# Moving the first attention's exponential to the eviction of the transposed scores, its maximum to GpSimd and its row sums to TensorE

## The reference

```python
Q = inputs @ Wq
K = inputs @ Wk
score = jnp.einsum('bqd,bkd->bqk', Q, K) / jnp.sqrt(jnp.float32(D))
score = jnp.where(causal, score, 0.0)
score = jnp.where(score != 0, score, NEG_FILL)   # finfo(float32).min
attn = jax.nn.softmax(score, axis=-1)
V = inputs @ (Wvdown @ Wvup)
return attn @ V
```

## Time and profile before

| what | value |
|---|---|
| median of 3 runs | 1756.0 us (1753.08 to 1756.61) |
| the profiled execution | 1755.23 us, span 1753.9 us |
| mean granted clock of TensorE in it | 0.977 |
| busy: PE / DVE / ACT / POOL | 1606.6 / 1491.6 / 1368.5 / 673.2 us |

### The profile page before, as it was taken

How to read it: one execution, slowest core, us unless ns; L and a number is a source line. 1 busy time by engine, 2 the same in 40 slices (tenths; PEclk the granted TensorE clock), 3 DMA queues, 4 the chain that set the end, 5 groups by cost and what they waited for, 6 DMA issues and landing times.

```text
span 1753.9 us, 54932 instructions
## 1 busy us (share of the span) xinstructions
PE 1606.6 (92%) x23271; PEld 662.3 (38%) x23281; DVE 1491.6 (85%) x2256; ACT 1368.5 (78%) x1934; POOL 673.2 (38%) x1085
## 2 busy tenths in 40 slices
PE   5768999999999999999999999999999999998998
PEld 2543343334334343334334343334433343222224
DVE  4648988899889988899889988899888988898973
ACT  4442688987899778887899878887798878786885
POOL 2321344435534454435454364434555262002010
PEclk9997799999999999999999999999999999998999
DMA  2120211112210311112210221112111222101111
GB/s 72 50 69 21 60 41 41 36 50 64 64 53 15 98 53 54 30 43 75 66 38 28 81 66 52 33 47 75 46 40 34 63 58 64 34 25 48 35 28 35
DMA packets 83281, 87.10 MB, mean 50 GB/s; under 512 B 9452, under 2 KB 67484, under 8 KB 83036
## 3 DMA queue, kind: packets, MB, share of 16 engines
q1 hardware_dynamic: 82492, 83.07, 16.1%
q10 hardware_dynamic: 544, 0.52, 0.1%
HBM read 61.02 MB, written 21.99 MB: 47 GB/s over the span
## 4 chain that ended last, share of the span: by engine, by line
PE 60%; ACT 18%; DVE 13%; issue 4%; SPq 2%; DMA 2%; POOL 1%; ACTq 0%; POOLq 0%
PE pv_psum L836 20%; PE side_psum L564 14%; ACT p L1049 11%; PE buffer L821 11%; DVE row_max L1367 7%; PE buffer L811 7%; PE side_psum L654 2%; PE buffer L564 2%; SPq L539 2%; PE side_psum L621 1%; ACT s L965 1%; ACT o_sb L1058 1%; DVE st_f L1112 1%; ACT hT_b L1038 1%; DVE s L1215 1%
## 5 line engine op out<-in xcount | busy, mean ns | idle before, releaser
L1367 DVE TENSOR_REDUCE row_max<-buffer 128x2 f32<-128x1024 f32 x1024 | 1234.3, 1219 | 150.0 <-PE buffer L811 137.8
L1049 ACT ACTIVATE p<-buffer 128x1024 f32<-128x1024 f32 x1024 | 1044.9, 1025 | 202.0 <-PE buffer L821 187.5
L836 PE MATMUL pv_psum<-p,v 128*9 128x256 f32 x8192 | 589.8, 384 | 10.5 <-ACT o_sb L1058 9.3
L811 PE MATMUL buffer<-k_ops,q_ops 24*128 24x512 f16 x2048 | 404.8, 392 | 35.9 <-ACT p L1049 26.1
L821 PE MATMUL buffer<-q_ops,k_ops 26*128 26x512 f16 x2048 | 401.3, 388 | 12.0 <-DVE row_max L1367 7.7
L836 PEld LDWEIGHTS pv_psum<-p,v 128*9 128x9 f32 x8192 | 150.0, 89 | 245.2 <-issue 162.0
L821 PEld LDWEIGHTS buffer<-q_ops,k_ops 26*128 26x128 f16 x2048 | 96.4, 91 | 382.2 <-issue 220.8
L1498 POOL TENSOR_TENSOR hm<-masks,hT_f 128x1024 f32<-128x1024 bf16 x56 | 120.3, 2148 | 103.1 <-PE side_psum L564 99.4
L811 PEld LDWEIGHTS buffer<-k_ops,q_ops 24*128 24x128 f16 x2048 | 96.6, 91 | 163.9 <-ACT p L1049 131.1
L1513 POOL TENSOR_SCALAR nm_parts<-nm 128x16 f16<-128x16 f32 x64 | 13.2, 207 | 298.1 <-DVE nm L1292 297.8
L564 PE MATMUL side_psum<-we,hm 128*32 128x128 f32 x3648 | 121.1, 274 | 2.4 <-issue 2.4
(11 more groups left out here) (309 smaller groups left out, 1617.6 us busy)
## 6 DMA issues: line engine op xcount, KB each, us to landing
masks<-masks_rows SPq DMA_DIRECT2D x16, 1024.0 KB, 6.3
q_ops<-products SPq DMA_DIRECT2D x256, 48.0 KB
k_ops<-products SPq DMA_DIRECT2D x256, 48.0 KB
attention<-o_sb SPq DMA_DIRECT2D x248, 18.0 KB
x<-in_L_attn_inputs SPq DMA_DIRECT2D x8, 512.0 KB, 4.4
products<-q_parts SPq DMA_DIRECT2D x16, 256.0 KB, 2.3
w_sb<-in_L_ffn_W SPq DMA_DIRECT2D x16, 256.0 KB, 3.3
out<-x SPq DMA_DIRECT2D x16, 256.0 KB, 2.4
```

Of the source, the lines that this page charges most:

```text
L811: m = e.matmul(buffer[:, hh, :], q_ops[rows, slot, of, i * P:(i + 1) * P], k_ops[rows, slot, of, halves(half)[1]], start=True, stop=True)
L836: m = e.matmul(pv_psum[q:q + VW, half * QUARTER:(half + 1) * QUARTER], v1[b % 2][:, kb, 2 * hp + hh, :], p_sb[n % KEPT][:, hh, part * QUAR ...
L1049: e.activation(p_sb[n % KEPT][:, :, :], unit("exp", n)[0][:, :, :], ACT.Exp, scale=over_scale[n // (2 * PERIOD)]).then_inc(S["exp_done"], 1)
L1367: e.tensor_reduce(mx[pair % 2][:, :, i, half], unit("max", n)[0][:, :, :], axis=AX.X, op=ALU.max).then_inc(S["max_done"], 1)
```

## The change

- `exp0` leaves ACT for all batches but the first. POOL does min(s - nm0, 1000) in place instead, and ACT's copy of the transposed block into `p0T` becomes exp(-x) of it. Batch 0 keeps ACT's exponential, without the sum.
- PE sums the rows: in `times_v`, for every key block and every 32 queries, a 128x32 weight of `p0T` is multiplied with a column of ones, into column 128 of the bank. Tiles 0 and 1, which use fewer than four column tiles, get matmuls with a column of zeros for the rest. `low` has 129 columns, and its copy takes all rows.
- `sums0` takes that column on POOL, in three operations instead of two, where nm0 shows that all was masked also the keys beyond. It now comes after `times_v` of tile 3 and 7 instead of after `exp0`.
- `exp0` has a gap of 2 steps instead of 1 and is no longer in `ON_ACT`.

Left out of the diff: the orders by hand of batches 0 and 1, from which `sums0` is moved in the same way, names of semaphores, memsets, and three waits of DVE's statistics for buffers that are long free.

```diff
@@ -90,9 +91,9 @@
             out += [(1, ("softmax", n - 1))]
         if n >= 3:
-            out += [(0, ("times_v", n - 3))] + ([(2, ("up", n // 7))] if n - 3 in (3, T - 1) else [])
+            out += [(0, ("times_v", n - 3))] + ([(0, ("sums0", n // 7)), (2, ("up", n // 7))] if n - 3 in (3, T - 1) else [])
         if 1 <= n < T + 1:
-            out += [(1, ("exp0", n - 1))] + ([(0, ("sums0", n // 5))] if n in (4, T) else [])
+            out += [(2, ("exp0", n - 1))]
         if n < T:
             out += [(0, ("scores", n, c)) for c in range(len(chunks(n)))]
@@ -138,7 +139,7 @@
 ZERO_TEST_ON_DVE = 2
 ON_DVE = {"stats", "softmax", "up", "wg", "top", "index", "onehot", "over_gating", "wff", "wout_mm", "stats_b", "ffn", "maxima"}
-ON_ACT = {"exp0", "gating"} | {name for name, by in EMPTIED_BY.items() if by == "act"} - {"nm"}
+ON_ACT = {"gating"} | {name for name, by in EMPTIED_BY.items() if by == "act"} - {"nm"}
 
 FRONT_FROM, WEIGHTS_FROM, BACK_FROM, LOAD_BEFORE = -200, 90, 132, 11
@@ -662,15 +663,21 @@
                 q = COLUMN_TILE * (j % 4)
                 weight, moving = (v0_later[:, i, :], pT[:, 0, :]) if k is None else (v0[:, k, :], pT[:, k + 1, :])
-                m = e.matmul(o[q:q + COLUMN_TILE, 0:P], weight, moving, start=j < 4, stop=j + 4 >= len(some))
+                e.matmul(o[q:q + COLUMN_TILE, 0:P], weight, moving, start=j < 4, stop=j + 4 >= len(some))
+            pe.wait_ge(S["zero_column"], 1)
+            for j in range(len(some), 4):
+                q = COLUMN_TILE * j
+                e.matmul(o[q:q + COLUMN_TILE, 0:P], zero_column[:, :].broadcast_to([P, COLUMN_TILE]), pT[:, 1, :], start=True, stop=True)
+            for k in range(i + 1):
+                for q in range(0, P, COLUMN_TILE):
+                    m = e.matmul(o[q:q + COLUMN_TILE, P:P + 1], pT[:, k + 1, q:q + COLUMN_TILE], ones_column[:, :], start=k == 0, stop=k == i)
             m.then_inc(S["side_filled"], 1)
 
...
             emptied("times_v", b, 4 * half + 3)
             pe.wait_ge(S["up_weights"], b + 1)
-            pe.wait_ge(S["low_zero"], 2)
-            four(v, lambda j: low[:, 4 * half + j, :], wvub[:, :])
+            four(v, lambda j: low[:, 4 * half + j, 0:P], wvub[:, :])
 
         def wg_stage(b, half):
@@ -944,10 +951,11 @@
 
         def times_v(b, i):
-            v, rows = filled("times_v", b, i), COLUMN_TILE * min(4, len(terms(i)))
+            v = filled("times_v", b, i)
             if b:
                 act.wait_ge(S["side_filled"], side["up", b - 1, i // 4].filled)
-            e.copy(low[0:rows, i, :], v[0:rows, 0:P]).then_inc(S["side_act"], 1)
+                act.wait_ge(S[f"over_sums0_{i // 4}"], b)
+            e.copy(low[:, i, :], v[:, 0:P + 1]).then_inc(S["side_act"], 1)
 
         def scores(b, i, c):
@@ -958,22 +966,23 @@
 
         def exp0(b, i):
+            if b:
+                return
             s, n = s0_of(b, i)[0], (i + 1) * P
             start = P if i == T - 1 else 0
             act.wait_ge(S["nm0"], b * T + i + 1)
-            act.wait_ge(S[f"over_sums0_{i // 4}"], b)
-            e.activation(s[:, start:P + n], s[:, start:P + n], ACT.Exp, scale=-1.0, bias=nm0[:, i:i + 1], accum_out=acc0[:, i:i + 1]).then_inc(S["p0"], 1)
-            if i % 4 == 3:
-                tiles = halves(i // 4)[0]
-                act.wait_ge(S["low_zero"], 2)
-                e.activation(e0[:, tiles], nm0[:, tiles], ACT.Exp, bias=neg[:, :]).then_inc(S[f"sums0_{i // 4}"], 1)
+            e.activation(s[:, start:P + n], s[:, start:P + n], ACT.Exp, scale=-1.0, bias=nm0[:, i:i + 1]).then_inc(S["p0"], 1)
 
         def transpose_p(b, i, c):
...
             if min(before) >= 0:
                 act.wait_ge(S["side_filled"], side["times_v", *before].filled)
-            e.copy(pT[:, some[0]:some[-1] + 1, :].rearrange("p k q -> p (k q)"), v[:, 0:len(some) * P]).then_inc(S["side_act"], 1)
+            pT = pT[:, some[0]:some[-1] + 1, :].rearrange("p k q -> p (k q)")
+            if b == 0:
+                e.copy(pT, v[:, 0:len(some) * P]).then_inc(S["side_act"], 1)
+                return
+            e.activation(pT, v[:, 0:len(some) * P], ACT.Exp, scale=-1.0).then_inc(S["side_act"], 1)
 
         def gating(b, half, part):
@@ -1436,12 +1449,14 @@
         def sums0(b, half):
             tiles = halves(half)[0]
-            pool.wait_ge(S[f"sums0_{half}"], b + 1)
-            pool.wait_ge(S["low_zero"], 2)
+            pool.wait_ge(S["nm0"], b * T + 4 * half + 4)
+            pool.wait_ge(S["low_zero"], 1)
             if b:
                 pool.wait_ge(S["side_dve"], side["up", b - 1, half].emptied)
-            after(e.tensor_tensor(rs0[:, tiles], e0[:, tiles], beyond[:, tiles], op=ALU.mult))
-            e.tensor_tensor(rs0[:, tiles], rs0[:, tiles], acc0[:, tiles], op=ALU.add).then_inc(S[f"over_sums0_{half}"], 1)
+            after(e.tensor_scalar(rs0[:, tiles], nm0[:, tiles], -NEG, 0.0, ALU.is_equal, ALU.add))
+            after(e.tensor_tensor(rs0[:, tiles], rs0[:, tiles], beyond[:, tiles], op=ALU.mult))
+            pool.wait_ge(S["side_act"], side["times_v", b, 4 * half + 3].emptied)
+            e.tensor_tensor(rs0[:, tiles], rs0[:, tiles], low[:, tiles, P], op=ALU.add).then_inc(S[f"over_sums0_{half}"], 1)
 
         def parts(b, w, half):
@@ -1480,6 +1495,14 @@
                 e.tensor_scalar(rest[:, 0:n], s[:, P:P + n], 0.0, -NEG, ALU.is_equal, ALU.mult).then_inc(S["masked"], 1)
 
+        def exp0(b, i):
+            if b == 0:
+                return
+            s, n = s0_of(b, i)[0], (i + 1) * P
+            start = P if i == T - 1 else 0
+            pool.wait_ge(S["nm0"], b * T + i + 1)
+            e.tensor_scalar(s[:, start:P + n], s[:, start:P + n], nm0[:, i:i + 1], NO_WEIGHT, ALU.subtract, ALU.min).then_inc(S["p0"], 1)
+
         def top(b, half, part):
             if not part:
```

More of the change, by code:

```diff
@@ L27 @@
 EPS = 1e-5
+NO_WEIGHT = 1000.0
 NEG = float(np.finfo(np.float32).min)
@@ L196 @@
 scores 0 1 0, softmax 0 0, exp0 0 0, stats 0 0 0 1, softmax 0 1, transpose_p 0 0 0, later 0, scores 0 2 0, exp0 0 1, times_v 0 0, transpose_p 0 1 0,
[L197 to L198 removed]
+softmax 0 2, scores 0 3 0, exp0 0 2, times_v 0 1, transpose_p 0 2 0, softmax 0 3, scores 0 4 0, exp0 0 3, scores 0 4 1, transpose_p 0 3 0,
+transpose_p 0 3 1, scores 0 5 0, exp0 0 4, softmax 0 4, scores 0 5 1, times_v 0 2, times_v 0 3, sums0 0 0, transpose_p 0 4 0, transpose_p 0 4 1, softmax 0 5,
 up 0 0, scores 0 6 0, exp0 0 5, stats 0 1 0 0, scores 0 6 1, times_v 0 4, stats 0 1 0 1, transpose_p 0 5 0, softmax 0 6, scores 0 7 0,
 transpose_p 0 5 1, exp0 0 6, scores 0 7 1, times_v 0 5, stats 1 0 0 0, transpose_p 0 6 0, channels 0 1 0, apply 0 1 0, softmax 0 7,
[L201 to L202 removed]
+transpose_p 0 6 1, exp0 0 7, wg 0 0, times_v 0 6, stats 1 0 0 1, transpose_p 0 7 0, top 0 0 0, stats 1 0 1 0, index 0 0 0,
+transpose_p 0 7 1, top 0 0 1, stats 1 0 1 1, times_v 0 7, sums0 0 1, index 0 0 1, squares 0, onehot 0 0, gating 0 0 0, up 0 1, gating 0 0 1, stats 0 1 1 0, apply 1 0 0,
 stats 0 1 1 1, onehotT 0 0, masks_out 0 0, over_gating 0 0, channels 0 1 1, apply 0 1 1, hm 0 0, apply 1 0 1, channels 1 0 0, limits 0, wg 0 1, inverse 0, top 0 1 0,
@@ L209 @@
 scores 1 2 0, channels 0 2 1, transpose_p 1 1 0, qk1 0 0 1, apply 0 2 1, softmax 1 2, parts 0 0 1, qk1 0 1 1, scores 1 3 0, v1 0 1, exp0 1 2,
-parts 0 1 1, transpose_p 1 2 0, times_v 1 1, sums0 1 0, exp0 1 3, scores 1 4 0, scores 1 4 1, transpose_p 1 3 0, transpose_p 1 3 1, softmax 1 3,
+parts 0 1 1, transpose_p 1 2 0, times_v 1 1, exp0 1 3, scores 1 4 0, scores 1 4 1, transpose_p 1 3 0, transpose_p 1 3 1, softmax 1 3,
 softmax 1 4, times_v 1 2, scores 1 5 0, exp0 1 4, scores 1 5 1, transpose_p 1 4 0, transpose_p 1 4 1, softmax 1 5"""
@@ L1132, in stats @@
                 dve.wait_ge(S[f"x2_{half}"], b + 1)
+            if which == 2:
+                dve.wait_ge(*norm("small", b, 1, half))
+            elif b:
+                dve.wait_ge(*norm("small", b - 1, 2 * which, half))
             st, mv = (st_f, mv_f) if which else (st_attn, mv_attn)
@@ L1344, in stats_b @@
             dve.wait_ge(S["side_dve"], side[("wout_mm", b, half) if b < B - 1 else ("last_wout", b, 1, half)].emptied)
+            if b:
+                dve.wait_ge(S["small_b"], 2 * (b - 1) + half + 1)
             norm_stats(xs[b % 4], st_b, mv_b, half, part, S["stats_b"])
@@ L1582, in inverse @@
             m.then_inc(S["powers"], 1)
-        stages = {"squares": squares, "inverse": inverse, "gates": gates_stage, "sums0": sums0, "stats": stats, "apply": apply, "parts": parts, "later": later, "scores": scores,
+        stages = {"squares": squares, "inverse": inverse, "gates": gates_stage, "sums0": sums0, "stats": stats, "apply": apply, "parts": parts, "later": later, "scores": scores, "exp0": exp0,
                   "top": top, "hm": hm_stage, "residual": residual, "nm_split": nm_split, "last_weights": last_weights_stage, "wout": wout_stage, "x_bias": x_bias, "numerators": numerators,
```

20 lines of the change are left out of this document (7 added, 13 removed).

## The result

The changed kernel takes 1789.05 us (median of 4, 1784.60 to 1791.76) against 1756.12 us before: 1.0195 times as long, 95% interval 1.0171 to 1.0218. The forecast was 1760, its range ended at 1776.

A forecast was written before the change was run, and what follows sets the result against it. TensorE was taken as the bound to 750 us in batch 4's block, VectorE from 757.7; -1.6 + 0.9 + 1.35 + 0.3 = +0.95 us a batch, six times +5.7, less 1 before the loop: 1760 us, range 1745 to 1776.

The forecast's parts named there:

- what ScalarE gives back: Steps where TensorE waits for ScalarE, up to 750 us in batch 4's block: -1.6 us a batch from the removed exponentials.
- the sums of tiles 0 to 3: Where TensorE is the bound: 80 one-column records and the zero matmuls add 0.9 us a batch.
- tiles 5 to 7: Where TensorE has 2.84 us free: 168 sum records, 1.45 us, delay transpositions by only +0.3 us a batch.
- The rate of GpSimd's subtraction: GpSimd's new exp0: 2.06 ns a column, 2.3 us at 1024 columns, bounds about 1.1 us and 3629 ns.
- that cover: Tile 7: subtraction ends at 762.9, transposition's place is 763.83, so no stall; at 3.6 us or more, late by 0.3.
- a rival at 0.10: GpSimd too slow at tile 7: subtraction ends 1.2 us after its place, 2.15 us a batch, 1767 us; chance 0.10.
- The clock: TensorE's granted clock in batch 4's block: read 1.00 throughout, the 2.4 GHz level; no term priced a fall.
- The wait at step 107: MoE first half's transposition, moved from step 112, waits for GpSimd's normalisation: +1.35 us a batch, bounds 0.8 and 1.6.
- The place before the loop: Batch 1: some 2 us of TensorE's wait behind exp0 go, sums cost about 1, together -1 us.
- The sums: TensorE's one-column matmuls: 288 records a batch at 8.6 ns each, 2.5 us, only partly on the path.
- The upper bound of 33 ns: Upper bound for one sum record, from tile 7's 16 records of 128 moving columns in 0.56 us; 9.5 us a batch.
- The rival on the sums: Sums cost a full group each, 25 ns a record: 3.65 us a batch, 1776 us; chance 0.10.

The follow-up runs named there:

- probe: The changed kernel plus seven forms of a 128x1024 fp32 GpSimd operation at step 900; multiply and add took 1124 ns, subtract alone 2852 ns.
- fast: The changed kernel with GpSimd's subtract and min replaced by multiply and add, masked scores marked 1e30: 1773.99 us, 1.0103 times the kernel before.
- busy2: The changed kernel with zero matmuls filling TensorE's waits at step 107 and tile 7 only, in the loop's six blocks: 1776.04 us, 1.0087 times the kernel before.
- busy: The changed kernel with zero matmuls ahead of the waits at step 107 and tile 7, and unintentionally at step 35: 1785.69 us, 1.0172 times the kernel before.
- late: The changed kernel with the transposition of the first expert half's normalised tiles back in step 112 from 107: 1769.88 us, 1.0065 times the kernel before.
- fast_late: The changed kernel with multiply and add on GpSimd and the normalised tiles' transposition back in step 112: 1752.01 us, 0.9974 times the kernel before.
- sums: The changed kernel with only TensorE's row sums kept, the exponential back on ScalarE, step table as before except sums0: 1760.95 us, 1.0039 times the kernel before.
- fast_late_few: The changed kernel with multiply and add, transposition in step 112, and only one key block of sums per tile (incomplete): 1744.69 us, 0.9932 times the kernel before.

## Why the prediction was wrong

The sum was +4.7 us, the profiled executions differ by 29.0. By the places of the table, forecast and measured over the six blocks: -4.2 and -0.4 up to step 103 (what ScalarE gives back, and the sums of tiles 0 to 3), +8.1 and +15.1 around step 107, +1.8 and +10.7 from step 112 on (tiles 5 to 7); before the loop -1 and +5.0, behind the blocks 0 and -1.3. So no single term failed. In the loop two did, the rate of GpSimd's subtraction and the price of a wait.

- *The rate of GpSimd's subtraction* is the step that failed at tile 7. It was taken at 2.06 ns a column from a 128-column add and multiply, so that tile 7 had cover and no stall; it was 3701 ns at 1024, just above the upper bound, the zero test at 3629. The row was chosen for its scalar from each partition and its fp32 output; the probe shows that the operations decide. The forecast had the consequence in a sentence ("if that cover goes (3.6 us or more) it is late by 0.3") and as a rival at 0.10, 1.2 us at tile 7. The wait was 1.63, and with the faster form alone (**fast**) the stretch went from 10.4 us to -0.7. The cover of tiles 0 to 6 was there: in the loop only tile 7's transposition waits for the subtraction.
- One rule of the Trainium skill bears on this: GPSIMD Engine Reference, section 4.1 Engine selection, has a row on elementwise add, mul and max by which work with one input runs at roughly line rate. Beside VectorE's 1.23 us for a row maximum over 1024 columns, the probe agrees for multiply and add, 1.12 us, and disagrees for subtract alone (2.85), min alone (2.77) and every other pair (3.65 to 3.72): the rule holds here for one form of seven.
- *The clock* was in no term: this step failed too. The prediction noted that it read 1.00 throughout and priced a wait at its length. After 1.36 us of idle TensorE the clock fell in three of six blocks, after tile 7's wait in four: 9.5 of 25.5 us, shown by busy2.
- *The wait at step 107* was right in place, cause and size: 1.3 forecast, 1.36 measured. But the sum gave the block +1.35 there, and without the lower clock that stretch cost 1.75 a block (10.5 / 6), with it 2.5 (15.1 / 6).
- *The place before the loop* came out with the other sign, +5.0 instead of -1; three more executions of the same program up to there (probe, busy, busy2) have +1.9, +3.4 and +3.9. The prediction looked at the wait of the earlier trace rows and not at what replaced it: in the change batch 1's transpositions wait for the subtraction there as well. But that is not shown to be the cause. **fast** has 1.6 us of these 8.3 us of waits left and still lost 3.9, **late** without the other wait 3.5, and only with both repairs (fast_late) is it +0.2; the mean clock of the first 183 us also differs, 0.87 in the change, 0.89 in probe and 0.85 in fast. The cause stays open.
- *What ScalarE gives back* was near in size and not where the forecast put it. From sums to fast_late, which differ by the exponential and by the step of exp0, the profiled executions gain 7.4 us (spans 1756.0 and 1748.6), against a forecast of 1.6 a block, 9.6, which counted the accumulator's reads as well. The forecast took it from TensorE's idle time up to step 107; of the gain, by the table, 2.1 us lie at steps 0 to 111 and 4.5 at steps 112 to 127. That the size is near is luck in part. That the exponential costs no more than the copy that it replaces was right: 597 ns against 589.
- *The sums* were near in total: 13 ns a record, not 8.6, and 7.3 us by fast_late_few for 224 records a batch, against 1.5 a block and 1 before the loop, 10 in all for 288. Their place was wrong: of the traces' 7.0 us 5.8 lie before the loop, where the forecast had 1, and tiles 0 to 3 cost nothing visible (steps 72 to 103 come out even, and fast_late_few, with 32 of their 80 records, loses no less there). The upper bound of 33 ns was misread: 0.56 us over 16 records are 35; nothing hangs on it. The rival on the sums, which ended at 1776, came nearest in time and was wrong in cause.
- The prediction's estimate by the Trainium skill, 7.2 us a batch, took the floor of about 25 ns (TensorE: Matmul & The Clock Gate, section Back-to-back issue gap) for every record, and the trace has 13 ns a record in four column tiles side by side. An fp32 matmul makes two records, so a one-column matmul took 26 ns, close to that figure. But v0's matmuls took 17 by the same count, so that this floor is what binds here is not shown.
